# A third layer's pass with stored bf16 one-hots, two sums a bank in the last layer, and an attention's end joined with its experts' norm

## The reference, cut to what matters

```
xn = layernorm(x);  x = x + gnn(xn, src, dst) + mix(xn);  x = x + ffn(layernorm(x))
```

```
h_prime = (x @ W + b).reshape(n, 8, 32)
e = leaky_relu((h_prime * a_src).sum(2)[src] + (h_prime * a_trg).sum(2)[trg], 0.2)
exp_e = exp(e - max(e))
denom = segment_sum(exp_e, trg);  alpha = exp_e / (denom[trg] + 1e-10)
out = segment_sum(h_prime[src] * alpha[:, :, None], trg)
```

## Time and profile before

| what | value |
|---|---|
| median of 3 runs | 5381.34 us (5380.28 to 5816.96) |
| the profiled execution | 5367.56 us |
| its span | 5365.8 us |
| PE busy | 4148.9 us (77%) |
| DVE busy | 3099.9 us (58%) |
| POOL busy | 2601.8 us (48%) |
| ACT busy | 1672.2 us (31%) |
| mean granted clock of PE | 0.870 |

### The profile page before, as it was taken

The page is one execution under the profiler, slowest core; times in us unless marked ns, Lnnn a source line. Parts: engine busy times, 40 slices in busy tenths (PEclk is TensorE's granted clock), DMA queues, the critical chain, the costliest instruction groups (busy, mean ns, idle before and its releaser), DMA issues. The chain is left out here.

```text
span 5365.8 us, 71878 instructions
## 1 busy us (share of the span) xinstructions
PE 4148.9 (77%) x19209; PEld 3079.2 (57%) x19209; DVE 3099.9 (58%) x7473; ACT 1672.2 (31%) x3813; POOL 2601.8 (48%) x2664
## 2 busy tenths in 40 slices
PE   1689997888976877559859678887499997888674
PEld 1357775656843544334548556666277765566564
DVE  5525546721057788779851467898522225688843
ACT  1345554532231322211333211000233334344221
POOL 1377775502206676548625367775000006777444
PEclk9799998988986777679969889888699999999877
DMA  5344447730028999857332344444100003333434
GB/s 176 117 150 156 155 148 229 220 104 27 31 87 281 328 329 320 268 157 230 91 115 71 95 128 122 122 120 89 48 0 0 0 5 116 103 101 97 94 101 128
DMA packets 463670, 705.71 MB, mean 132 GB/s; under 512 B 70819, under 2 KB 340649, under 8 KB 462923
## 3 DMA queue, kind: packets, MB, share of 16 engines
q0 software_dynamic: 115216, 335.54, 20.8%
q1 hardware_dynamic: 327133, 344.61, 20.5%
q10 hardware_dynamic: 20978, 21.42, 1.3%
HBM read 496.93 MB, written 205.25 MB: 131 GB/s over the span
## 5 line engine op out<-in xcount | busy, mean ns | idle before, releaser
L830 POOL DMA_INDIRECT m_rows<-support,edge x440 | 445.6, 1013 | 878.9 <-POOLq L129 737.1
L3404 POOL DMA_INDIRECT g_sc_rows<-keyval,src_at x440 | 430.3, 978 | 321.0 <-POOLq L129 107.3
L4014 POOL DMA_INDIRECT g_sp_rows<-h,src_at x440 | 469.8, 1068 | 145.9 <-issue 97.2
L2210 POOL DMA_INDIRECT messages<-m_rows,place_at x440 | 429.8, 977 | 154.8 <-issue 96.0
L3423 PE MATMUL g_sc_pair<-g1q_parts,g_sc_near 125*128 x1320 | 289.5, 341 | 145.9 <-DVE g_sc_rows L3455 112.6
L4063 PE MATMUL g_sp_bank<-g_sp_rows,g_sp_same 128*125 128x264 f32 x880 | 287.8, 435 | 73.3 <-DVE g_total L4203 68.7
L1391 DVE SCALAR_TENSOR_TENSOR x<-f_y,f_comb,x 125x256 f32 x200 | 96.8, 484 | 377.9 <-PE f_y L1208 377.9
L851 PE MATMUL m_half<-m_rows,m_marks 128*125 128x256 f32 x880 | 240.8, 408 | 70.3 <-issue 33.6
L3639 POOL TENSOR_TENSOR g_sp_rows<-g_sp_rows,g_alpha 128x512 f32<-128x512 f32 x220 | 225.0, 1043 | 126.2 <-DMA g_sp_rows<-kept 122.7
L1250 ACT ACTIVATE f_hid<-f_h,f_shift,f_scale 128x375 f32<-128x375 f32 (+1 forms) x320 | 195.5, 611 | 288.9 <-PE f_h L1187 283.2
L3650 PE MATMUL g_sp_bank<-g_sp_rows,g_sp_same 128*125 128x260 f32 x880 | 263.5, 421 | 17.2 <-POOL g_sp_rows L3639 10.7
(11 more groups left out here) (734 smaller groups left out, 10425.7 us busy)
## 6 DMA issues: line engine op xcount, KB each, us to landing
g_sums_rows<-messages SPq DMA_DIRECT2D x110, 520.0 KB
kept<-g_sc_rows SPq DMA_DIRECT2D x440, 128.0 KB, 9.1
g_sp_rows<-kept SPq DMA_DIRECT2D x440, 128.0 KB, 2.6
answer_rows<-zero ACTq DMA_DIRECT2D x1, 14592.0 KB
g_sc_which<-kind_rows SPq DMA_DIRECT2D x55, 256.0 KB
m_local_in<-local_rows SPq DMA_DIRECT2D x55, 252.0 KB
near_rows<-m_near SPq DMA_DIRECT2D x55, 252.0 KB
g_sc_near<-near_rows SPq DMA_DIRECT2D x55, 250.0 KB
```

The costliest lines, as they stand in the source:

```text
L830: nc.gpsimd.indirect_dma_start(self.rows[:, k, :], None, self.table, bass.IndirectOffsetOnAxis(ap=core.far_at[:, s:s + 1], axis=0)).then_i ...
L2210: nc.gpsimd.indirect_dma_start(core.messages, bass.IndirectOffsetOnAxis(ap=core.place_at[:, s:s + 1], axis=0), self.rows[:, k, :], None).t ...
L3404: nc.gpsimd.indirect_dma_start(rows[:, k, :], None, table, bass.IndirectOffsetOnAxis(ap=core.src_at[:, s:s + 1], axis=0)).then_inc(gathere ...
L4014: nc.gpsimd.indirect_dma_start(self.rows[:, k, :], None, self.table, bass.IndirectOffsetOnAxis(ap=core.src_at[:, s:s + 1], axis=0)).then_i ...
```

## The change

It has four parts.

**1. The third layer's pass.** The one-hots `near` are no longer made. The first layer already writes the same one-hots in bf16 to device memory (`near_rows`, with a row 125 that is 1 for pads), and SP loads a group of them (126 x 1024, bf16) into one of three buffers. The target logits are split into three bf16 parts before the pass (`parts`, with a row of -1e30 for the pads, which replaces `gone`), so that `expand_pe` is one bf16 product of 24 columns. The parts are added by a reduction out of PSUM, and the wait for the gathered rows moves one step later. `match` moves from DVE to ACT, as eight Square activations of 128x125 and one Relu of 128x1000 a group, two groups ahead, with three groups held.

```diff
-            sp.dma_start(self.local_in[:, g % 2, :], self.core.local_rows[mine].partition_broadcast(P)).then_inc(self.marked[g % 2], 16)
+            if g >= self.HELD:
+                sp.wait_ge(self.expanded, GROUP * (g - self.HELD + 1))
+            sp.dma_start(self.near[:, g % self.HELD, :], self.core.near_rows[g]).then_inc(self.near_in[g % self.HELD], 16)
...
-        nc.tensor.matmul(self.near_bank[:, k * heads:(k + 1) * heads], self.near[:, g % 2, k * W:(k + 1) * W],
-                         self.target[:, bass.ds(tile, 1), :].rearrange("p o h -> p (o h)"), start=True, stop=True).then_inc(self.expanded, 1)
+        nc.tensor.matmul(self.near_bank[:, k * width:(k + 1) * width], self.near[:, g % self.HELD, k * W:(k + 1) * W],
+                         self.parts[0:P + 1, bass.ds(tile, 1), :, :].rearrange("p o i h -> p (o i h)"), start=True, stop=True).then_inc(self.expanded, 1)
...
+    def match(self, act, g):
+        nc = self.core.nc
+        there = self.same[:, g % self.HELD]
+        if g >= self.HELD:
+            act.wait_ge(self.summed, GROUP * (g - self.HELD + 1))
+        for k in range(GROUP):
+            s = g * GROUP + k
+            ins = nc.scalar.activation(there[:, k, :], self.core.ramp[:, 0:P], ACT.Square, bias=self.minus_local[:, s:s + 1])
+        ins.then_inc(self.apart, 1)
+        act.wait_ge(self.apart, g + 1)
+        nc.scalar.activation(there, there, ACT.Relu, scale=-1.0, bias=self.one[:, 0:1]).then_inc(self.same_set, 1)
...
+    def step_act(self, act, s):
+        g, k = s // GROUP, s % GROUP
+        if k == 0 and 0 < g < GROUPS - 1:
+            self.grow_act(act, g + 1)
+        if k == 3 and g + 2 < GROUPS:
+            self.match(act, g + 2)
...
-        if k == 3 and g + 1 < GROUPS:
-            self.match(v, g + 1)
-        if k == 5 and g + 4 < GROUPS:
-            self.mark(v, g + 4)
...
+            spread = self.near_bank[:, 0:GROUP * self.PARTS * heads].rearrange("p (s i h) -> p s h i", i=self.PARTS, h=heads)
+            nc.vector.tensor_reduce(z, spread, AX.X, ALU.add).then_inc(self.taken, 1)
         elif part == 1:
+            for s in range(g * GROUP, (g + 1) * GROUP):
+                v.wait_ge(self.gathered[s % self.SLOTS], 16 * (s // self.SLOTS + 1))
             v.wait_ge(self.taken, g + 1)
+            nc.vector.tensor_tensor(z, z, self.rows[:, self.slots(g), D:D + heads], ALU.add).then_inc(self.joined, 1)
```

```diff
-        if s >= slots:
-            pe.wait_ge(self.added, s - slots + 1)
+        if s % 2 == 0 and s >= slots:
+            pe.wait_ge(self.added, s - slots + 2)
...
-        v.wait_ge(self.summed, s + 1)
+        v.wait_ge(self.summed, s // 2 * 2 + 2)
...
-            sums.place(ph, [half[0:P, 0:D] for half in halves])
+            sums.place(ph, [half[0:P, j * D:(j + 1) * D] for half in halves for j in range(2)])
```

```diff
+        def _(sp):
+            sp.dma_start(tile_i[:], core.tile_row.partition_broadcast(P)).then_inc(tiles_in, 16)
+            fetch(sp)
+            sp.wait_ge(tiles_in, 16)
...
+        def _(pool):
+            pool.wait_ge(shared_out, 1)
+            for o in range(NODE_LOOPS):
+                there = by_head(tiles(hprime, o))
+                nc.gpsimd.tensor_tensor(there, there, bcast_last(tiles(mine, o), wide), ALU.mult).then_inc(own_scaled, 1)
+                pool.wait_ge(own_scaled, o + 1)
+                pool.wait_ge(sum_added, o + 1)
+                nc.gpsimd.tensor_tensor(tiles(core.x, o), tiles(core.x, o), tiles(hprime, o), ALU.add).then_inc(own_added, 1)
...
+            def add_sums(o):
+                there = by_head(tiles(total, o)[:, :, 0:D])
+                nc.vector.tensor_tensor(there, there, bcast_last(tiles(part, o), wide), ALU.mult).then_inc(sum_scaled, 1)
+                v.wait_ge(sum_scaled, o + 1)
+                nc.vector.tensor_tensor(tiles(core.x, o), tiles(core.x, o), tiles(total, o)[:, :, 0:D], ALU.add).then_inc(sum_added, 1)
...
+            for o in range(AHEAD):
+                add_sums(o)
+            for o in range(NODE_LOOPS):
+                v.wait_ge(own_added, o + 1)
+                for t in range(o * BODY, (o + 1) * BODY):
+                    norm.tile_stats(v, t)
+                norm.spread(v, link, o)
+                if o + AHEAD < NODE_LOOPS:
+                    add_sums(o + AHEAD)
+                norm.refine(v, link, o)
...
+        ffn2(core, lambda fetch: gnn2_end(core, attend, hprime, total, own, heads, fetch))
```

More of the change, by code:

```diff
@@ L1109, in ffn, with fetch @@
         nload = 16 * len(loads)
-        with nc.Block() as prefetch:
-            @prefetch.sync
-            def _(sp):
-                for to, what in loads:
-                    sp.dma_start(to, what).then_inc(loaded, 16)
-        if before:
-            before()
+        def fetch(sp):
+            for to, what in loads:
+                sp.dma_start(to, what).then_inc(loaded, 16)
+        before(fetch)
         hbank = [ph.ps(f"h{i}") for i in range(HR)]
@@ L2767, in ffn2 @@
         norm={"w": "L2_ffn_W2", "eps": 1e-3, "columns": [[f"L2_ffn_{n}{i}" for n in ("b", "g", "be", "m", "v")] for i in (1, 2)]},
-        before=lambda: layer_norm(core, "ln2b", core.x, None, core.xnT, rows=False))
+        before=before)
 def gnn3_front(core, table):
@@ L4040, in begin_pe @@
         self.spread_pe(pe, -1)
+        pe.wait_ge(self.split, self.PARTS)
         for g in range(3):
@@ L4085, in begin @@
         self.chain(nc.vector.memset(self.ones[:], 1.0))
-        self.chain(nc.vector.tensor_scalar(self.gone[:], core.local[:], 0.0, self.LOW, ALU.is_lt, ALU.mult))
         self.link(nc.vector.memset(self.best[:], self.LOW))
-        self.link(nc.vector.memset(self.total[:], 0.0))
         self.link(nc.vector.tensor_reduce(self.best[0:P, :], own, AX.XY, ALU.max))
+        self.chain(nc.vector.memset(self.parts[96:W, :, 0, :], self.LOW))
+        self.link(nc.vector.memset(self.parts[96:W, :, 1:self.PARTS, :], 0.0))
+        for i in range(self.PARTS):
+            part = self.parts[0:P, :, i, :]
+            nc.vector.tensor_copy(part, self.target).then_inc(self.split, 1)
+            if i < self.PARTS - 1:
+                v.wait_ge(self.split, i + 1)
+                self.link(nc.vector.tensor_tensor(self.target, self.target, part, ALU.subtract))
+        nc.vector.memset(self.one[:], 1.0).then_inc(self.placed, 1)
+        nc.vector.tensor_scalar(self.minus_local[:], core.local[:], -1.0, None, ALU.mult).then_inc(self.placed, 1)
         nc.vector.tensor_scalar(self.diag[:], core.ident[:], self.best[:, 0:1], None, ALU.mult).then_inc(self.diag_set, 1)
@@ L4094, in begin @@
         self.tiles = StepTiles(v, "attend", core.step_tile)
-        self.mark(v, 0)
-        self.mark(v, 1)
+        self.link(nc.vector.memset(self.total[:], 0.0))
         self.logits(v, 0)
@@ L4099, in begin @@
         self.negate(v, 0)
-        self.mark(v, 2)
         self.logits(v, 1)
@@ L4103, in begin @@
         self.negate(v, 1)
-        self.mark(v, 3)
-        self.match(v, 0)
         self.tiles.load(0)
```

306 lines of the change are left out of this document (86 added, 220 removed).

## The result

| | before | after |
|---|---|---|
| median | 5382.4 us (4 runs) | 5317.1 us (4 runs) |
| profiled execution | 5367.6 | 5315.4 |
| span | 5365.8 | 5313.6 |

The ratio is 0.9873, with a 95% interval from 0.9859 to 0.9887, which is 61 to 76 us faster; the medians differ by 65. Forecast was 5330, and 5317 was measured. One of the four executions of the kernel before took 5817 us and is left out of the ratio. The two profiled executions differ by 52 us. Both kernels go through the same order of stages, so the 52 can be laid out by milestones of the two traces (first and last gather of each pass, the first instruction of the attention's end, the row of `mine`, the experts' first product). The other 13 of the 65 can't be placed, as each kernel has one trace.

The account below looks back on a forecast made before the run. The prediction took POOL's gather issue to bound the third layer's pass. Its terms, -28 - 2 - 6 + 1 - 16 = -51 from 5367.6, gave 5316.6, and with 13.8 to the median 5330 us; range 5285 to 5375.

Parts of the forecast that it names:

- The bound and the floor: Third layer's pass: gather issue sets the pace, 550 us at the median gather, 56 us excess from large DVE operations.
- Part 1: Third layer's pass: marks and comparisons leave DVE, so gathers are held up less, -28 us (bounds 0 and -56).
- the prediction's rate from the last layer's pass: Last layer's gathers: 0.39 us lost per DVE comparison, carried to the third layer as -21, with marks -35.
- The scalings hold the gathers: Rival, third layer's pass: row scalings cause most of the hold-up, so -14 instead of -28, 5344 us; chance 0.15.
- The -2 of the tail: Behind the third layer's last gather: two matches leave DVE's busy queue, -2 us.
- The additions: Third layer's pass: ACT's new operations, 233 us in all, fit into its idle time and cost 0 (bounds 0 and 4).
- the rival that needed 0.71: Third layer's pass: PE's clock falls below 0.71, PE becomes the bound and the kernel slower, 5401 at 0.65; chance 0.05.
- The 100 us that PE was to lose: Third layer's pass: fp32 expansion leaves PE, some 100 of 505 us, leaving it busy about 405.
- Part 4: Attention's end joined with the norm, split between DVE and POOL running one after the other: 76 us to 69, -6.
- the rival of free overlap (-31): Rival, attention's end: POOL's and DVE's operations run side by side, -31 instead of -6, 5305 us; chance 0.17.
- Part 2: Last layer's sums: six PSUM buffers shorten PE's wait for a bank, -8 in gathers and -8 behind them, -16 us.
- Part 3: Last layer's loads split so PE can begin earlier; gathers set the pace, so 0 (bounds 0 and -4).

Follow-up runs that it names:

- e5: The changed kernel with the third layer's row scalings cut to one column of 512, leaving work out: 5286.4 us.
- e6: The changed kernel with POOL's two operations a group in the attention's end moved to DVE: 5307.1 us in one execution.
- e7: The changed kernel with the last layer's comparison taken off DVE, its weighed marks made on ACT by Square and Relu: 5293.4 us in one execution.
- e8: The kernel before with the third layer's pass changed, but its scatter comparison left on DVE: 5365.8 us against 5390.3.
- e1: The kernel before with only the third layer's pass changed (stored bf16 one-hots, comparison on ACT): 5828.6 us against 5844.6, ratio 0.9974.

## Why the prediction was right

*The bound and the floor.* That the pass is paced by the issue of its gathers, with a floor of 550 us, and that DVE's large operations make the excess of 56, is shown by e5 (549.9, with no gather above 0.992). This was the step on which the rest stood.

*Part 1: -28 forecast, -26 measured* (-33 with e6's and e7's pass of 572.6). The size was right and its division wrong. By the prediction's rate from the last layer's pass the comparison had 21 of 35; by the runs it has 0 to 7 once the marks are gone (579.5 against 572.6 to 579.7), and the marks have the rest. The rate itself was sound in the stage from which it was taken: -21 was worked out there, and e7 measured -22 (-19 and -21 against e5 and e6 on its own chip). What failed is the transfer to a stage with a third kind of large operation, in which collisions aren't a sum over operations. "The scalings hold the gathers" was half right as well: they hold what is left, 23 to 30 us, and yet the change gained 26. The -2 of the tail didn't come: DVE is busy 24.3 us there instead of 28.9, and the stretch is as long as before.

*The additions.* ACT's 233 us cost nothing, as forecast (187 more in the window and no new wait on `same`; e5's floor leaves no room for one). The clock fell from 0.88 to 0.86 in the pass, and the rival that needed 0.71 didn't occur. The 100 us that PE was to lose in the pass were 62 (504.8 to 442.9), which cost nothing, as PE is not the bound.

*Part 4: -6 forecast, -13 measured,* the term that was most mis-sized. "One after the other" holds, and the rival of free overlap (-31) is out. But 69 laid all of POOL's and DVE's work end to end, and from `mine` to the last copy it is 3742.4 to 3805.8, 63 us. POOL's price was near: ten operations at 2.75 make 27.5, and they were busy 28.4, or 26.1 at the 2.34 and 2.88 that they take when nothing holds them. That is 1.4 of the 5.4 missing (68.7 in the sum, 63.3 measured), and the other 4 are work that did overlap: a product of POOL takes 3.59 beside DVE's statistics, which then are done too. Without POOL's operations nothing can overlap, and there the same kind of sum came out: 20 x 1.49 + 8.6 + 12.5 + 5.5 = 56.4 against 56.3 measured to the last copy (e6).

*Part 2: -16 forecast, -16 measured,* in other proportions (3 and 13 for 8 and 8). Against e8 it is 8 to 10 and 12 to 13, so the 8 of the gathers may have been right. Part 3, put at 0, can have a share of the 13. The lag of PE's sum behind the gather shows why. Before, the sum of step 350 ended 30.8 us after its gather and the last one 19.7 after; with the change 11.5 and 8.9. So the tail lost 11 us of lag. The 7 us of POOL's own waits did go. But PE's idle time fell only from 57 to 46 us, not under 25: most of it wasn't the wait for a bank, and the label of ACT's marks, which the prediction argued away, has 24.7 us beside 24.8 before.

*The total.* -51 for the profiled executions, and they differ by 52. That close a match is luck: four stretches of the table gained less than forecast, by 3, 2, 2 and 5 us, and three gained more, by 7, 1 and 5, and these cancel. The medians differ by 65: the 13.8 us between profiled execution and median, which the prediction carried over, were 1.7 for the changed kernel. That was a property of one execution, not of the kernel.

## What to carry to other kernels

Where GpSimd's indirect DMAs set the pace, look at the gathers' distribution, not their mean: the median gives the floor, and what is above it belongs to large DVE operations beside them. Don't price such collisions one by one where several kinds share the stage: take each kind away alone and see. And an engine whose operations go one after the other with those of the busy one is no help: POOL's share of the attention's end cost 7 us more than DVE doing it all.

## What the runs showed of the hardware

- A DVE operation with one input (bf16 in, fp32 out, 125x1024, 0.76 us) held up 49 of 440 indirect DMAs, 0.23 us each, and one with two fp32 inputs held them as well (e5, e8): a gather beside the scalings took up to 1.50 us, against 0.99 without them (e5). A held gather lost 0.23 us (marks) to 0.32 (comparisons) on average and 0.92 at most (1.871 less 0.948), short of the 1.19 of the comparison. The Trainium skill ("SBUF — State Buffer", "SBUF: two separate sides") counts the operations with two inputs only against a GpSimd operation that reads on-chip memory. The gather does read its row numbers from there (`src_at`), so the traces agree; no run has a gather that doesn't.
- An operation of 125x5 on DVE took 2.73 us beside a POOL addition of 125x1280, and 0.17 without one.
- On two of the three chips of these runs a step of 128 rows took 1.5 to 1.6 us in place of 1.3, and the kernel before 5799 and 5845 us in place of 5390. The gathers landed as quickly there, but PE's sums lagged by all 32 slots, and in e1's pass all four engines stood still for 38 us. Whether this belongs to the chip, and what it is, is open. There part 1 gave 15 us, and PSUM room in the last layer 12 to 18 us in the gathers, where the chip of e5 to e8 shows 8 to 10.
